# Decoder block on one Trainium2 core: q and k stored stacked and laid out by four DMAs a group, row maxima by way of DRAM, inverse of the softmax sums on ScalarE

## The chip, the cores and the metric

One core of a Trainium2 chip runs the whole program in one launch. The metric is the device time in microseconds (us); lower is better. Engines: PE is TensorE, ACT is ScalarE, DVE is VectorE, POOL is GpSimd, and SP is SyncE, which here only waits and issues DMAs.

## The reference, cut to what matters

```python
x = x + mixer(layernorm(x))                    # linear, conv, scan, gates; B=8, L=256, D=256
q = layernorm(x) @ WQ + bQ;  k = ctx @ WK + bK;  v = ctx @ WV + bV      # 16 heads of 16
scores = where(causal, einsum('bhqd,bhkd->bhqk', q, k) * SCALE, -inf)
x = x + (softmax(scores) @ v) @ WO + bO
x = x + top2_of_8_experts(layernorm(x))        # capacity 641 a expert, hidden 1024
```

The attention is exact in fp32 to a small tolerance. So q and k are held as two parts, high and low (`qkh`, `qkl`, type fp32r), and a product is high*high + high*low + low*high.

## The kernel before, in words

There are three stages: the mixer with the projections (`mixer_and_projections`), the attention with routing, and the experts (both in `attention_route_experts`). No scheduler works here: each engine has a queue written out by hand, and semaphores join them.

At the end of the mixer, q and k of each block of 512 tokens go to DRAM: `store` (L262) writes the high part to `qd[0]` or `kd[0]` and the low part to `qd[1]` or `kd[1]`, one DMA of 512 KB each. The stage ends when SP has seen all of them land (L309 to L312).

The attention works on 16 groups (GR). A group is one batch of 256 tokens and 8 of the 16 heads. For each group SP does two things:

- `lay(g)` (L1074) fills `q3` and `k3`. Per head they hold 48 rows: for q the parts high, high, low, for k high, low, high, so that one matmul of 48 rows gives the three products. Six 16-row pieces of q and six of k are loaded, each by a DMA of its own (L1082): 12 DMAs a group. `ITEMS` is 4 buffers, and `lay(g)` waits until group g-4 is used up (semaphore `st`).
- `maxima(g)` (L1085) waits for the row maxima in `mt` (semaphore `ml`) and writes them, again as high and low, into two extra rows of `q3`, one head a DMA (L1091): 16 DMAs of 1 KB a group. With -1 in the two extra rows of `k3` the next product has the maximum already subtracted.

The compute engines walk through steps t, three per group, 48 in all (NS). PE at step t does in this order: `turned_mask(t)` (L1375, waits for the exponential of t-1), `mask(u)` (L1350) and `scores(u)` (L1363) with u = t + LEAD and LEAD = 6, between these two `turned(t)` (L1389, keys by queries, 50 rows), and `weigh(t-1)` (L1411, probabilities times v and times ones). `turned(3g)` is the only one that waits for the maxima of group g. DVE reduces the scores of u to maxima (`maxima`, L1574). `turn_maxima(g)` on PE (L1424), `maxima_high` on ACT (L1248) and `maxima_low` on DVE (L1578) bring them into row form at step 3g-3. ACT computes the exponential (`exps`, L1243) of step t into one of three buffers `pr`. There is one PSUM buffer for the turned scores and one for the scores. After step 3g+2 of a group DVE divides (`divide`, L1583 and L1586): a reciprocal of the sums, then a product.

Every six steps a batch is projected (`project`, L1439); every twelve steps a block of four groups is normed (`normed`, L1253), turned (L1451), and gets logits (L1462), the choice of experts (`choose`), ranks (`ranks`, `place`) and its scatters to the experts' buffers in DRAM (`scatter` on POOL, L1173). The numbers NORM, TURN, LOGITS, RANKS, SEND in L998 are the steps at which this is due. The experts start when all scatters have landed.

## Time and profile before

| | |
|---|---|
| median of 3 runs | 905.03 us (902.49 to 905.58) |
| profiled execution, own time | 904.72 us |
| its span, first to last instruction | 903.0 us |
| mean granted PE clock | 0.858 |
| PE busy | 678.1 us (75%) |
| DVE busy | 508.2 us (56%) |
| ACT busy | 346.5 us (38%) |
| POOL busy | 325.3 us (36%) |
| DMA packets, bytes | 65987, 76.81 MB |

The page gives busy time by engine, the busy share in 40 slices, and the chain of work that ended last, followed back from the last instruction. SP has no row of busy time; what it does shows only in the chain and in the timeline, as "SPq" with a line number. Times in the timeline count from the first instruction. A clock of 1.00 is the upper level of PE (2.4 GHz), 0.50 the lower (1.2 GHz).

### The profile page before, as it was taken

What the parts mean: (1) busy time and instruction counts of PE and PEld (TensorE: products, weight loads), DVE (VectorE), ACT (ScalarE), POOL (GpSimd) and SP (SyncE); (2) the same over time, 40 slices, a digit from 0 to 9 for tenths busy, and PEclk for the clock granted to TensorE, in tenths of its full rate; (3) what the DMA queues carried; (4) which work ended last, traced back from release to release, by engine and by line L of the source; (5) the groups of instructions that cost most, each with busy time, mean ns of one, the idle gap of its engine ahead of it and who ended that gap; (6) DMA issues with size and microseconds to landing.
All of it is one profiled execution on the core that took longest, in us unless ns stands there. A gap on an engine that the chain in (4) does not pass through costs nothing.

```text
span 903.0 us, 13776 instructions
## 1 busy us (share of the span) xinstructions
PE 678.1 (75%) x4984; PEld 561.2 (62%) x4984; DVE 508.2 (56%) x985; ACT 346.5 (38%) x674; POOL 325.3 (36%) x307
## 2 busy tenths in 40 slices
PE   3869989798642357667667857733999999999992
PEld 2548877687431134344344535423999999999992
DVE  6686877869431224444544533422678777787741
ACT  4555647244310022223223213112556556565541
POOL 1326232423007000001113013052457776866855
PEclk9889999999875566879977878755999999999997
DMA  9002056211213632222323311115043454351213
GB/s 293 16 25 94 24 189 211 97 48 52 88 46 95 198 109 57 60 75 57 92 53 112 89 50 58 31 32 186 1 130 62 107 144 96 75 144 17 31 20 40
DMA packets 65987, 76.81 MB, mean 85 GB/s; under 512 B 17739, under 2 KB 52566, under 8 KB 65920
## 3 DMA queue, kind: packets, MB, share of 16 engines
q1 hardware_dynamic: 56704, 68.12, 23.8%
q0 software_dynamic: 9216, 7.81, 6.1%
q8 instruction: 40, 0.66, 0.3%
q14 instruction: 27, 0.22, 0.1%
HBM read 47.75 MB, written 29.64 MB: 86 GB/s over the span
## 4 chain that ended last, share of the span: by engine, by line
SPq 28%; PE 28%; issue 6%; POOL 4%; DMA 2%; DVE 1%; ACT 1%; POOLq 0%
SPq L1091 17%; PE w_bank L1516 13%; PE w_bank L101 11%; SPq L1082 10%; POOL out L1197 2%; PE w_bank L1485 1%; DMA a_q<-a_mt 1%; POOL a_k L1204 1%; POOL disp L1173 1%; POOL w_hl L1186 1%; DMA w_rows<-disp 1%; PE a_turned L1389 0%; DMA out<-w_y,w_to 0%; PE a_out L1411 0%; PE a_shared L1462 0%
## 5 line engine op out<-in xcount | busy, mean ns | idle before, releaser
L1574 DVE TENSOR_REDUCE a_nm<-a_scores 128x4 f32<-128x1024 f32 (+1 forms) x48 | 58.6, 1221 | 158.4 <-PE a_scores L1363 158.4
L1243 ACT ACTIVATE a_pr<-a_turned 128x1024 f32<-128x1024 f32 x48 | 49.2, 1025 | 197.5 <-PE a_turned L1389 197.5
L1516 PE MATMUL w_bank<-w_w2h,w_hh 128*108 128x256 f32 x384 | 108.6, 283 | 1.3 <-POOL w_hl L1186 1.3
L1516 PE MATMUL w_bank<-w_w2h,w_hl 128*108 128x256 f32 x384 | 107.8, 281 | 0.0
L1516 PE MATMUL w_bank<-w_w2l,w_hh 128*108 128x256 f32 x384 | 107.5, 280 | 0.0
L1677 DVE SCALAR_TENSOR_TENSOR w_v<-w_th,w_bank 128x324 f32<-128x324 f32 x128 | 62.8, 492 | 70.2 <-ACT w_th L1281 68.4
L1180 POOL TENSOR_TENSOR w_w1l<-w_s,w_w1h 128x256 fp32r<-128x256 f32 x64 | 56.7, 886 | 120.1 <-ACT w_w1h L1270 120.1
L1281 ACT ACTIVATE w_th<-w_bank 128x324 f32<-128x324 f32 x128 | 56.6, 443 | 99.8 <-PE w_bank L101 98.0
L1389 PE MATMUL a_turned<-a_q,a_k 50*128 50x256 f32 (+1 forms) x256 | 33.2, 364 | 81.9 <-DMA a_q<-a_mt 81.9
L1186 POOL TENSOR_TENSOR w_hl<-w_v,w_hh 128x324 fp32r<-128x324 f32 x64 | 56.5, 882 | 91.4 <-ACT w_hh L1287 91.4
L1389 PEld LDWEIGHTS a_turned<-a_q,a_k 50*128 50x128 f32 x256 | 22.3, 228 | 99.4 <-DMA a_q<-a_mt 90.2
L101 PE MATMUL w_bank<-w_xh,w_w1h 128*128 128x324 f32 x256 | 80.5, 315 | 1.1 <-ACT w_xh L1276 1.1
L101 PE MATMUL w_bank<-w_xh,w_w1l 128*128 128x324 f32 x256 | 80.1, 313 | 0.0
L1197 POOL DMA_INDIRECT out<-w_y,w_to x48 | 75.4, 1570 | 13.2 <-issue 9.9
L101 PE MATMUL w_bank<-w_xl,w_w1h 128*128 128x324 f32 x256 | 80.1, 313 | 0.0
L1653 DVE TENSOR_TENSOR w_w2l<-w_s,w_w2h 128x256 fp32r<-128x256 f32 x64 | 66.2, 1035 | 2.2
L1516 PEld LDWEIGHTS w_bank<-w_w2h,w_hh 128*108 128x108 f32 x384 | 65.8, 171 | 1.8 <-issue 1.8
L1516 PEld LDWEIGHTS w_bank<-w_w2l,w_hh 128*108 128x108 f32 x384 | 66.0, 172 | 0.0
L1516 PEld LDWEIGHTS w_bank<-w_w2h,w_hl 128*108 128x108 f32 x384 | 65.9, 172 | 0.0
L1287 ACT ACTIVATE w_hh<-w_v 128x324 fp32r<-128x324 f32 x128 | 60.3, 472 | 12.0 <-DVE w_v L1677 11.0
L101 PE MATMUL m_bank<-m_sh,m_wh 128*128 128x512 f32 x112 | 46.6, 416 | 10.3 <-ACT m_sh L422 6.9
L1173 POOL DMA_INDIRECT disp<-w_x,w_si x32 | 31.7, 990 | 58.8 <-DVE w_si L1646 46.3
(211 smaller groups left out, 1686.3 us busy)
## 6 DMA issues: line engine op xcount, KB each, us to landing
w_s<-in_L_ffn_w SPq DMA_DIRECT2D x16, 1024.0 KB, 5.0
a_q<-qd SPq DMA_DIRECT2D x96, 64.0 KB, 3.2
a_k<-kd SPq DMA_DIRECT2D x96, 64.0 KB, 2.3
disp<-c_blank SPq DMA_DIRECT2D x8, 658.1 KB
w_rows<-disp SPq DMA_DIRECT2D x8, 658.1 KB
vd<-m_vf SPq DMA_DIRECT2D x4, 1024.0 KB, 4.5
a_v<-vd SPq DMA_DIRECT2D x8, 512.0 KB, 4.2
a_q<-a_mt SPq DMA_DIRECT2D x256, 1.0 KB
```

Source lines behind the costliest of these rows:

```text
L101: mm = pe.matmul(out, a, b, start=first and n == 0, stop=last and n == 3 * len(parts) - 1)
L1082: sp.dma_start(m[at:at + HD, :, :].bitcast(F32), heads[e])\
L1091: sp.dma_start(q3[g % ITEMS][at:at + 1, p, :].bitcast(F32), mt[g % 2][h:h + 1, n, :].bitcast(F32))\
L1180: pool.tensor_tensor(w1_piece(w1l, f), w1_piece(s1[e % 2], f), w1_piece(w1h, f).bitcast(F32), ALU.subtract)\
L1186: pool.tensor_tensor(hl[:, g % 3, half(1)], v[:, n % 4, :], hh[:, g % 3, half(1)].bitcast(F32), ALU.subtract)\
L1197: pool.indirect_dma_start(out=out, out_offset=bass.IndirectOffsetOnAxis(ap=to[:, e % 3, t:t + 1], axis=0), in_=y[e % 2][:, t, :], in_offse ...
L1281: act.activation(th[:, n % 2, :], hb[n % 3][:, 0:HALF], ACT.Tanh, scale=0.5).then_inc(F["th"], 1)
L1287: act.activation(hh[:, g % 3, half(u)], v[:, n % 4, :], ACT.Copy).then_inc(F["hh"], 1)
L1516: mm = pe.matmul(eb[t // 2][0:SP_, (t % 2) * D:(t % 2 + 1) * D], a[:, g % 3, s], w2_piece(b, f), start=f == 0 and t % 2 == 0 and n == 0, s ...
L1574: dve.tensor_reduce(dst, src, AX.X, ALU.max).then_inc(A["nm"], 1)
L1653: dve.tensor_tensor(w2_piece(w2l, f), w2_piece(s2[e % 2], f), w2_piece(w2h, f).bitcast(F32), ALU.subtract)\
L1677: dve.scalar_tensor_tensor(v[:, n % 4, :], th[:, n % 2, :], 1.0, hb[n % 3][:, 0:HALF], ALU.add, ALU.mult).then_inc(F["v"], 1)
```

## The change

- In DRAM, q and k are now stacked as `lay` wants them: `qd` and `kd` have 3*D rows, and `store` writes high, high, low (q) or high, low, high (k), for two halves of 64 partitions: 6 DMAs of 256 KB in place of 2 of 512 KB, the high or the high and low part twice over. The weights' columns are reordered on the host (`by_pair`), so that the heads fall in the right place.
- `lay(g)` loads 48 rows at once: 4 DMAs of 192 KB in place of 12 of 64 KB.
- `maxima(g)` writes `mt` to a DRAM tensor `md` with one DMA, waits for it, and reads it back into the rows of `q3` with two DMAs of 2 rows: 3 in place of 16.
- LEAD is 7 in place of 6, and `turn_maxima`, `maxima_high` and `maxima_low` of group g come at step 3g-4 in place of 3g-3. LOGITS is 21 (was 20), RANKS 24 (23), SEND 25 (24).
- The inverse of the sums is made by ACT (`inverse`): a logarithm, then an exponential of minus that. DVE keeps the product.
- `values` and `store_base` are issued at other groups by SP.

```diff
@@ store
-                    for m, part in enumerate((qkh, qkl)):
-                        sp.dma_start(dst[m][:, i * BLK:(i + 1) * BLK].rearrange("(k p) t -> p k t", p=P),
-                                     part[:, :, :].bitcast(F32)).then_inc(S[sem], 16)
+                    for e in range(2):
+                        for n, part in enumerate((qkh, qkh, qkl) if dst is qd else (qkh, qkl, qkh)):
+                            sp.dma_start(dst.rearrange("(k e s q) n -> e s q k n", k=DC, e=2, s=3)[e, n][:, :, i * BLK:(i + 1) * BLK],
+                                         part[64 * e:64 * e + 64, :, :].bitcast(F32)).then_inc(S[sem], 16)
@@ lay and maxima, on SP
-                    for m, srcs in ((q3[g % ITEMS], (qd[0], qd[0], qd[1])), (k3[g % ITEMS], (kd[0], kd[1], kd[0]))):
-                        for n, src in enumerate(srcs):
-                            heads = src[k * P:(k + 1) * P, b * L:(b + 1) * L].rearrange("(p e r) t -> e r p t", p=4, e=2)
-                            for e in range(2):
-                                at = 64 * e + HD * n
-                                sp.dma_start(m[at:at + HD, :, :].bitcast(F32), heads[e])\
-                                    .then_inc(A[f"laid{g % ITEMS}"], 16)
+                    for m, src in ((q3[g % ITEMS], qd), (k3[g % ITEMS], kd)):
+                        rows = src.rearrange("(k e s r p) n -> k e (s r) p n", k=DC, e=2, s=3, r=HD)
+                        for e in range(2):
+                            sp.dma_start(m[64 * e:64 * e + 3 * HD, :, :].bitcast(F32), rows[k, e][:, :, b * L:(b + 1) * L])\
+                                .then_inc(A[f"laid{g % ITEMS}"], 16)
...
-                    for n in range(2):
-                        for e in range(2):
-                            for p in range(4):
-                                at, h = 64 * e + 3 * HD + n, 4 * e + p
-                                sp.dma_start(q3[g % ITEMS][at:at + 1, p, :].bitcast(F32), mt[g % 2][h:h + 1, n, :].bitcast(F32))\
-                                    .then_inc(A[f"m_in{g % 2}"], 16)
+                    sp.dma_start(md.rearrange("(g n h) t -> g h n t", n=2, h=8)[g], mt[g % 2][:, :, :].bitcast(F32)).then_inc(A["md"], 16)
+                    sp.wait_ge(A["md"], 16 * (g + 1))
+                    for e in range(2):
+                        at = 64 * e + 3 * HD
+                        sp.dma_start(q3[g % ITEMS][at:at + 2, :, :].bitcast(F32),
+                                     md.rearrange("(g n e p) t -> g e n p t", n=2, e=2, p=4)[g, e]).then_inc(A[f"m_in{g % 2}"], 16)
@@ ACT
+                def inverse(g):
+                    act.wait_ge(A["pv"], 3 * g + 3)
+                    ge(act, A["o"], g)
+                    act.activation(rc[:, :], obank[g % 2][:, L:2 * L], ACT.Ln).then_inc(A["ln"], 1)
+                    act.wait_ge(A["ln"], g + 1)
+                    act.activation(rc[:, :], rc[:, :], ACT.Exp, scale=-1.0).then_inc(A["rc"], 1)
...
+                act.preload_act_table_set("natural_log_exp_and_others")
                 maxima_high(0)
+                maxima_high(1)
                 for t in range(END):
+                    if t % 3 == 0 and 1 <= t // 3 <= GR:
+                        inverse(t // 3 - 1)
                     if t < NS:
                         exps(t)
-                    if t % 3 == 0 and t // 3 + 1 < GR:
-                        maxima_high(t // 3 + 1)
+                    if t % 3 == 2 and (t + 4) // 3 < GR:
+                        maxima_high((t + 4) // 3)
@@ DVE, divide
-                    dve.wait_ge(A["pv"], 3 * g + 3)
-                    step(dve.reciprocal(rc[:, :], obank[g % 2][:, L:2 * L]))
-                    settled()
+                    dve.wait_ge(A["rc"], g + 1)
```

The same shift from `t % 3 == 0` to `t % 3 == 2` stands for `turn_maxima` on PE and `maxima_low` on DVE. How the queues read now is shown at three places.

ACT, from the start of the attention into group 2: first before, then the change. `a_pr` is the exponential, `a_mt` the maxima, `a_rc` the inverse, `w_w1h` a piece of an expert's weight.

```order
L1248 ACTIVATE a_mt<-a_shared 8x256 [waits a_mT]
L1243 ACTIVATE a_pr<-a_turned 128x1024 [waits a_st]
L1248 ACTIVATE a_mt<-a_shared 8x256 [waits a_mT]
L1243 ACTIVATE a_pr<-a_turned 128x1024 [waits a_st] x2
L1270 ACTIVATE w_w1h<-w_s_0 128x2x128 [waits f_s1_0]
L1243 ACTIVATE a_pr<-a_turned 128x1024 [waits a_pv,a_st]
L1248 ACTIVATE a_mt<-a_shared 8x256 [waits a_m_in0,a_mT]
L1243 ACTIVATE a_pr<-a_turned 128x1024 [waits a_pv,a_st] x3
```

```order
L1306 ACT_TABLE_LOAD
L1248 ACTIVATE a_mt<-a_shared 8x256 [waits a_mT] x2
L1243 ACTIVATE a_pr<-a_turned 128x1024 [waits a_st] x3
L1248 ACTIVATE a_mt<-a_shared 8x256 [waits a_md,a_mT]
L1277 ACTIVATE w_w1h<-w_s_0 128x2x128 [waits f_s1_0]
L1253 ACTIVATE a_rc<-a_out 128x256 [waits a_pv]
L1255 ACTIVATE a_rc<-a_rc 128x256 [waits a_ln]
L1243 ACTIVATE a_pr<-a_turned 128x1024 [waits a_pv,a_st] x3
L1248 ACTIVATE a_mt<-a_shared 8x256 [waits a_md,a_mT]
```

The two instructions on `a_rc` stand ahead of the first exponential of the next group, and they wait for `a_pv`, the last products of the group before.

SP, one group in the steady part: first before, then the change.

```order
L1082 DMA a_q_1<-qd 16x4x256 [waits a_st]
L1082 DMA a_q_1<-qd 16x4x256 x5
L1082 DMA a_k_1<-kd 16x4x256 x6
L1091 DMA a_q_3<-a_mt 1x16x16 [waits a_ml]
L1091 DMA a_q_3<-a_mt 1x16x16 x15
```

```order
L1081 DMA a_q_1<-qd 48x4x256 [waits a_st]
L1081 DMA a_q_1<-qd 48x4x256
L1081 DMA a_k_1<-kd 48x4x256 x2
L1086 DMA md<-a_mt 8x2x256 [waits a_ml]
L1090 DMA a_q_3<-md 2x1024 [waits a_md]
L1090 DMA a_q_3<-md 2x1024
```

28 DMAs have become 7, and a wait on a DMA (`a_md`) stands inside.

PE in the change, the first step of a group: where `turned` waits for the maxima, and what stands between it and the next exponential.

```order
L1400 MATMUL a_turned<-a_q_1,a_k_1 128x256 [waits a_m_in1]
L1400 MATMUL a_turned<-a_q_1,a_k_1 128x256 x3
L1374 MATMUL a_scores<-a_k_3,a_q_3 128x256 x4
L1422 MATMUL a_out<-a_pr,a_v_0 32x128 [waits a_exp]
L1422 MATMUL a_out<-a_pr,a_v_0 32x128 x3
L1422 MATMUL a_out<-a_pr,a_ones 32x128 x4
L1422 MATMUL a_out<-a_pr,a_v_0 32x128 x4
L1422 MATMUL a_out<-a_pr,a_ones 32x128 x4
L1386 MATMUL a_turned<-c_identb,c_mask 128x2x128 [waits a_exp]
```

The transposes of the maxima (L1424 before) no longer stand in this step; they have moved to the step ahead of it, the third step of the group before.

## Rows read from the trace of the kernel before

**Rows 1.** The page, part 4: the chain that ended last, by line

```profile
SPq L1091 17%; PE w_bank L1516 13%; PE w_bank L101 11%; SPq L1082 10%; POOL out L1197 2%; PE w_bank L1485 1%; DMA a_q<-a_mt 1%; POOL a_k L1204 1%; POOL disp L1173 1%; POOL w_hl L1186 1%; DMA w_rows<-disp 1%; PE a_turned L1389 0%; DMA out<-w
```

**Rows 2.** Timeline of SP, one group: start, duration, queue, line, DMA, count

```profile
402.35 2.82 SPq L1082 DMA_DIRECT2D a_q<-qd  x6
...
408.84 9.99 SPq L1091 DMA_DIRECT2D a_q<-a_mt  x16
418.87 3.59 SPq L1082 DMA_DIRECT2D a_q<-qd  x6
```

**Rows 3.** Timeline of PE, one group without a wait for SP (idle time in brackets)

```profile
419.94 0.50 PE L1389 MATMUL a_turned<-a_q,a_k 50*128 50x256 f32 x4 [3.39 <-DMA a_q<-a_mt]
...
424.29 0.50 PE L1389 MATMUL a_turned<-a_q,a_k 50*128 50x256 f32 x4
...
426.08 1.99 PE L1439 MATMUL a_shared<-w_wo,a_ot 128*128 128x256 f32 x8
427.91 1.85 PE L1462 MATMUL a_shared<-w_rw,w_xt 128*128 128x8 f32 x16
429.62 0.59 PE L1375 MATMUL a_turned<-c_identb,c_mask 128*128 128x512 bf16 x2
...
430.36 0.66 PE L1389 MATMUL a_turned<-a_q,a_k 50*128 50x128 f32 x8
...
432.24 0.39 PE L1375 MATMUL a_turned<-c_identb,c_mask 128*128 128x256 bf16 x2
```

**Rows 4.** Stretches: busy (xcount) of PE, PEld, DVE, ACT, POOL; PE clock, DMA share, GB/s

```profile
409.00:412.00 3.00, 0.53 (x7) 0.33 (x4) 1.50 (x3) 1.50 (x4) 0.00 (x0) 1.00 0.15 44
421.00:423.00 2.00, 2.00 (x36) 1.67 (x35) 1.64 (x2) 1.46 (x4) 0.00 (x0) 0.50 0.39 110
280.00:300.00 20.00, 8.14 (x40) 4.26 (x40) 6.51 (x6) 0.37 (x1) 8.56 (x4) 0.50 0.47 144
320.00:572.00 252.00, 175.37 (x1768) 112.60 (x1768) 112.83 (x219) 63.69 (x89) 31.96 (x30) 0.79 0.27 73
```

**Rows 5.** Timeline of PE: the turn of a normed block

```profile
411.68 0.66 PE L1451 MATMUL a_shared<-c_ident,w_x 128*128 128x128 f32 x4 [2.47 <-ACT w_x L1253]
```

**Rows 6.** Groups of the page, ACT and DVE (busy us, mean ns | idle)

```profile
L1574 DVE TENSOR_REDUCE a_nm<-a_scores 128x4 f32<-128x1024 f32 (+1 forms) x48 | 58.6, 1221 | 158.4 <-PE a_scores L1363 158.4
L1243 ACT ACTIVATE a_pr<-a_turned 128x1024 f32<-128x1024 f32 x48 | 49.2, 1025 | 197.5 <-PE a_turned L1389 197.5
...
L1281 ACT ACTIVATE w_th<-w_bank 128x324 f32<-128x324 f32 x128 | 56.6, 443 | 99.8 <-PE w_bank L101 98.0
```

**Rows 7.** Timelines of SP and PE, end of the mixer and start of the attention

```profile
266.69 0.47 SPq L265 DMA_DIRECT2D qd<-m_qkl  x1
...
278.81 2.68 SPq L1082 DMA_DIRECT2D a_q<-qd  x6
...
286.25 1.12 PE L1363 MATMUL a_scores<-a_k,a_q 48*128 48x128 f32 x8 [14.35 <-DMA a_k<-kd]
...
300.62 0.79 PE L1363 MATMUL a_scores<-a_k,a_q 48*128 48x256 f32 x4
...
320.45 0.80 PE L1389 MATMUL a_turned<-a_q,a_k 50*128 50x256 f32 x4 [16.68 <-DMA a_q<-a_mt]
```

**Rows 8.** DMA landings: page part 6 (KB, us to landing), and one in the chain

```profile
a_q<-qd SPq DMA_DIRECT2D x96, 64.0 KB, 3.2
...
kd<-m_qkl SPq DMA_DIRECT2D x4, 512.0 KB, 3.9
...
434.73 1.64 DMA a_q<-a_mt
```

**Rows 9.** Timelines of PE and DVE, the last group; the chain at the first product

```profile
571.53 0.80 PE L1389 MATMUL a_turned<-a_q,a_k 50*128 50x256 f32 x4 [2.40 <-DMA a_q<-a_mt]
...
582.48 1.76 DVE L1583 RECIPROCAL a_rc<-a_out 128x256 f32<-128x256 f32 x1 [3.76 <-PE a_out L1411]
...
625.60 3.43 PE w_bank L101 x12
```

60 lines of the change are left out of this document (33 added, 27 removed).

## The prediction

> **What bounds the kernel now.** I read the chain that ended last first. SP's queue is the largest holder of the span: L1091 and L1082, the DMAs of the maxima and of q and k, hold 17% and 10% of it [rows 1], some 245 us. No other work of the attention is over 1%. The timeline of SP shows why: one group takes 6 issues for q in 2.82 us, as many for k up to 408.8, and 16 for the maxima in 9.99, with no idle time between, and the next group's first issue comes 16.5 us after this one's [rows 2]. So SP's own issuing is the bound: some 0.47 us an issue for a 64 KB piece, 0.62 us for a 1 KB row. The other engines wait: PE stands 3.39 us before the first product of a group until the maxima have landed [rows 3]. The attention proper, from the first `turned` at 320.45 [rows 7] to that of the last group at 571.53 [rows 9], is 251.1 us for 15 groups, 16.7 each. The mixer and the experts do not hang on this queue.
>
> The second thing to read is what a group costs once SP does not hold it. The timeline of PE has one that runs from its first product to the next group's masks with hardly a pause [rows 3].
>
> **What the change removes.** 28 issues a group become 7. The four large ones I take at 0.47 us; the issue time hardly follows the bytes, since the 512 KB store is issued in 0.47 too [rows 7]. The three for the maxima take 0.6 each. SP then needs 1.9 + 1.8 us and one landing between, 6 to 8 us a group [rows 8], and is no longer the bound. What is late next is PE.
>
> **Three steps of PE, at the upper clock.** Second step: from `turned` at 424.29 to the projection at 426.08, 1.79, plus the masks ahead of the next `turned`, 429.62 to 430.36, 0.74: 2.53. Third step: 430.36 to 432.24, 1.88, plus 0.74: 2.62. First step: 419.94 to 424.29, 4.35, but of this some 2.7 us ran at clock 0.50 [rows 4]; at 1.00 these are 1.35, so 3.0. Together 8.2 us [rows 3].
>
> **What the change adds on this path.** `inverse` stands on ACT ahead of `exps(3g+3)`, and it waits for the 32 small products of step 3g+2, the last thing PE does in that step. Before, that exponential ran beside those products. Now PE has nothing left: after the products come about 0.1 us to reach ACT, the logarithm, the exponential, the next exponential of 1024 columns at 1.02 [rows 6], and 0.15 back. No row shows a logarithm of 256 columns. Two rows of ACT give the slope: 443 ns for 324 columns and 1025 for 1024 [rows 6], 0.83 ns a column, so 0.39 for 256. Both ends: 0.3 and 0.45 each. I take 0.4 twice, and so 2.1 us of standing PE a group. On DVE 1.76 us of reciprocal [rows 9] go away, 16 times. That is 28 us of an engine with idle time, and I cost it at nothing: its reduces take 1.22 us each [rows 6], and what hides them is PE's work of a step.
>
> **The rest of the steps.** A projection is 1.83 us (426.08 to 427.91) and the logits 1.71 (to 429.62) [rows 3]. The turn of a normed block is twice 0.5 with a wait of 2.47 for ACT [rows 5] and some 0.4 for the second half: 3.9. Up to the last group these are 7 projections, 3 logits, 3 turns and 0.6 of ranks: 12.8 + 5.1 + 11.7 + 0.6 = 30.2, or 2.0 a group. So the **period is 8.2 + 2.1 + 2.0 = 12.3 us** in place of 16.7.
>
> **The maxima's way.** With LEAD 7 and `turn_maxima` at 3g-4, four steps lie between it and `turned(3g)`: the rest of one (1.0), a first step with its pause (5.1), a second and third (5.2) and masks (0.7), 12.0 us without projections. Needed are 1.9 for the copy and the subtraction (which stands behind a reduce), 0.6 to issue, a landing in DRAM, 1.2 for two issues, a landing in SBUF. Landings run from 1.64 (a 1 KB row) over 3.2 (64 KB of q) to 3.9 (512 KB written to DRAM) [rows 8]. That is 7.0 to 11.5; I take 8.5, hidden. The four loads of `lay` sit just ahead in the same queue, which argues for the upper half.
> The Trainium skill (page "DMA: Bandwidth & Descriptors", section on the anatomy of one DMA) speaks against the detour: a DMA has a fixed cost of about 2.0 us, most of it the receipt of the last write, worst where HBM is written; two trips would be 4.0 or more, which by its figure also leaves them hidden. No row here shows a small write to DRAM.
>
> **The start.** The last store of q is 6 issues in place of 2: four more at 0.47, +2 us before the mixer can end (at least 0.8, at most 4.5 if the bytes, 1.5 MB for 1, count in full). POOL's memsets follow as before, so `lay(0)` starts at 280.8. Four issues (1.9) and a landing near 3.2 give the first scores at 285.8, where they were at 286.25 [rows 7]. Steps run there at clock 0.50 [rows 4], and 5 of them took 14.37 us (286.25 to 300.62), 2.87 each. Seven are 20.1, so the first `turned` comes at 306.0 in place of 320.45. The other stores of the mixer double their high part behind some 2 us more of issue. The next writer of `qkh` asks for them more than 8 us later, so I cost them at nothing; without that cover it would be 2 us a block.
>
> **The end.** In the last group the inverse of group 14 stands ahead of an exponential, +2.1, and 0.8 us of ACT replace 1.76 on DVE, -0.9: +1.2. Ranks and scatters one step later fall into idle time of POOL.
> Two table loads are new on ACT. One falls under POOL's memsets. The other stands ahead of the experts' first tanh, while PE works on the first product for 3.43 us [rows 9], so nothing.
> By the Trainium skill ("ScalarE: Activation LUTs", what ACT_TABLE_LOAD costs) a switch is about 2.66 us, still under that; its price is on no row here.
>
> **The sum.** Last group's `turned` at 306.0 + 15 x 12.3 = 490.5, in place of 571.5: -81.0, and +1.2 at the end: -79.8. From the profiled execution's own 904.72 that gives **825 us**. The median of the three runs is 905.03, 0.3 above it, which I leave out.
>
> **The rivals.**
>
> *The low clock stays in the period* (20%). Today PE drops to 0.50 after its long pause in a group: idle before 419.94, it runs at 0.50 from 421 to 423, while the 2.47 us pause before 411.68 left it at 1.00 [rows 3 to 5]. The new pauses are 2.1 to 2.5, like the one that did no harm; that speaks against it. Several of them close together, with micro-pauses in the 50-row products, speak for it. If one low stretch of 2.7 us a group stays, it costs 1.35 or, with projections in it, up to 1.8: period 13.7 to 14.1, 846 to 852 us.
> The Trainium skill ("TensorE: Matmul & The Clock Gate", Part 1) says that the clock follows how busy PE has lately been, down to half when idle; by that rule denser work should end the drops and give the 825, and the pause of 2.47 us agrees with it.
>
> *The maxima are late after all* (8%). If both landings take 4.5 or more behind the loads, 12.7 to 16 are needed and the period grows by 1 to 2.5: 840 to 863 us. PE would again wait for the DMA at the first `turned` of a group.
>
> *More falls into the shadow* (5%). The 2.1 us pause also lets DVE, ACT and the norm's chain catch up, so that the 2.9 us waits of the turns and the masks' waits vanish, and some masks are already issued: period 11.2, 808 us.
>
> *The change does not relieve SP* (1%). If an issue were priced by its rows, 48 for 16, four would cost 1.41 each, 5.6 as today, and SP would need 5.6 + 1.8 + 3: 10.4, still under 12.3. Only with waits behind full queues on top does it bind, near 16: 880 to 903.
>
> *Slower: the pauses keep PE at the lower clock* (3%). In the first 20 us of the attention short bursts with pauses ran at 0.50 throughout [rows 4]. At 0.50 in every step, the 8.2 become 16.4 and the 1.1 of projections and logits in the 2.0 double: 21.6 a group, 15 x 9.3 = 140 more than the sum, 965 us. It needs a period of 17.6 to be slower than before, 5.3 over mine on 9.4 of PE's work, so the low level for over half of the time. Today, with longer pauses, the mean over the attention is 0.79 [rows 4], the low level for 42% of it.
>
> **The numbers.** The forecast has 63%, within 813 to 840: the period from 11.6 (some of the waits above shared) to 13.1, the start up to 3 us later. The range takes in the low clock: **812 to 857**. About 0.3%, 2.7 us, is what a measurement of this kernel can tell from no change. Faster 0.96, same 0.01, slower 0.03.
>
> **What would show it.** Right: SP's two lines have left the chain, and PE or ACT hold it between 306 and 490; the first product of a group follows the last by 12 to 13 us; ACT's logarithm waits for the small products, and PE's mask of the next step waits for the exponential, about 2 us, 16 times; `turned` has no wait for a DMA. Wrong: `turned` waits for the read of `md`, or the clock in the attention is under 0.8, or the period is over 14 or under 11.5; a first product far from 306 would show a fault in the start.

## The result and the profile after

| | before | after |
|---|---|---|
| median of 4 runs | 905.31 us (902.49 to 906.53) | 837.47 us (833.26 to 845.19) |
| the profiled execution, its span | 904.72 us, 903.0 | 833.26 us, 831.5 |
| mean granted clock of PE | 0.858 | 0.891 |
| first `turned` of the first and of the last group, us | 320.45, 571.53 | 312.55, 501.38 |
| period of a group (from first `turned` to the next group's, mean of 15) | 16.74 | 12.59 |
| from the last group's first `turned` to the end | 331.5 | 330.1 |

The ratio is 0.926, with a 95% interval of 0.918 to 0.935: 7.4% faster, or 67.8 us between the medians. Forecast were 825 (812 to 857). Of the 71.5 us between the two spans, 7.9 were won at the start, 62.3 in the period and 1.3 behind. The four runs of the change lie further apart (1.4%) than those of before (0.4%), and their mean clocks, 0.891 and 0.887 for the two at 833, 0.880 for 841.5 and 0.876 for 845.2, fall as the times rise.

The page of after, the chain by engine and by line, against [rows 1]:

```profile
PE 46%; issue 5%; POOL 4%; ACT 4%; DVE 3%; DMA 2%; SPq 2%; another core or an unknown queue 1%; POOLq 0%; ACTq 0%
PE w_bank L1527 14%; PE w_bank L101 12%; PE a_out L1422 5%; PE a_turned L1400 3%; PE a_turned L1386 2%; PE a_shared L1450 2%; POOL out L1197 2%; ACT a_pr L1243 2%; PE a_scores L1361 1%; PE a_scores L1374 1%; SPq L1081 1%; PE w_bank L1496 1%; PE a_shared L1473 1%; DVE a_nm L1585 1%; DMA md<-a_mt 1%
```

SP's two lines held 27% of the span; all of SP now holds 2%. In their place stand PE's own products of the attention (L1422, L1400, L1386).

Timeline of SP in after, one group and the next group's loads, against [rows 2]:

```profile
403.31 1.19 SPq L1081 DMA_DIRECT2D a_q<-qd  x2
404.54 1.25 SPq L1081 DMA_DIRECT2D a_k<-kd  x2
405.83 0.50 SPq L1086 DMA_DIRECT2D md<-a_mt  x1
409.37 0.54 SPq L1090 DMA_DIRECT2D a_q<-md  x2
416.94 1.19 SPq L1081 DMA_DIRECT2D a_q<-qd  x2
```

Four loads take 2.5 us (0.62 each, not 0.47), the maxima 0.50 and 0.54, and between write and reads lie 3.0 us of waiting for the landing. From 403.31 to 409.91 SP is at it, and then it stands idle for 7.0 us.

Timeline of PE in after over the same group, against [rows 3] (the first row, from the group before, is for comparison with that of 411.15):

```profile
399.49 0.64 PE L1422 MATMUL a_out<-a_pr,a_v 128*32 128x256 f32 x8
...
406.08 0.50 PE L1400 MATMUL a_turned<-a_q,a_k 50*128 50x256 f32 x4
...
409.69 0.39 PE L1386 MATMUL a_turned<-c_identb,c_mask 128*128 128x256 bf16 x2 [1.86 <-ACT a_pr L1243]
...
411.15 1.08 PE L1422 MATMUL a_out<-a_pr,a_v 128*32 128x256 f32 x8
```

The 3.39 us in front of a group's first product, for the maxima, are gone. In their place is a pause of 1.86 us behind the small products, and after it eight products take 1.08 us that take 0.64 at 399.49: PE has fallen to the lower clock (0.51 from 410.5 to 414.0). Not every such pause is followed by a fall: the row at 399.49 stands behind one of 1.86 us too, that of the group before, and there the clock stayed up. The timeline of ACT shows what fills it:

```profile
407.89 0.38 ACT L1253 ACTIVATE a_rc<-a_out 128x256 f32<-128x256 f32 x1 [3.24 <-PE a_out L1422]
408.31 0.42 ACT L1255 ACTIVATE a_rc<-a_rc 128x256 f32<-128x256 f32 x1
408.63 1.00 ACT L1243 ACTIVATE a_pr<-a_turned 128x1024 f32<-128x1024 f32 x1
```

Logarithm 0.38, exponential of 256 columns 0.42, then the exponential that PE waits for. The waits of the whole execution, of PE and of ACT (us in total, times, longest), say how often this is so:

```profile
PE a_turned L1386 <- ACT a_pr L1243: 31.1, 16, 4.3
...
ACT a_rc L1253 <- PE a_out L1422: 48.1, 15, 4.9
```

Fifteen of PE's 16 waits are the inverse's: 14 of 1.86 to 1.91 us, and one of 4.30 ahead of 491.68, where ACT's logarithm began 2.5 us after the last product, held by something that the trace calls only "remote". The sixteenth, 0.69, is in the first group, where no inverse stands ahead yet.

Stretches of after, against [rows 4] (busy of PE, PEld, DVE, ACT, POOL, then PE's clock, DMA share, GB/s):

```profile
290.00:300.00 10.00, 5.71 (x30) 3.25 (x30) 3.67 (x3) 0.00 (x0) 3.83 (x2) 0.50 1.01 232
300.00:312.00 12.00, 7.78 (x36) 3.32 (x34) 5.72 (x6) 0.74 (x2) 0.00 (x0) 0.50 0.86 269
320.00:470.00 150.00, 122.61 (x1448) 79.09 (x1446) 71.33 (x157) 58.00 (x94) 21.65 (x21) 0.92 0.37 100
```

In the attention the clock rose to 0.92, so PE is at 0.50 for some 16% of the time in place of 42%; the low stretches have not gone. The start ran as low as before.

The start, in the timelines of SP and PE of after, against [rows 7]:

```profile
266.57 1.23 SPq L266 DMA_DIRECT2D qd<-m_qkh  x2
...
268.58 2.54 SPq L266 DMA_DIRECT2D qd<-m_qkh  x2
271.17 1.18 SPq L266 DMA_DIRECT2D qd<-m_qkl  x1
284.07 1.26 SPq L1081 DMA_DIRECT2D a_q<-qd  x2
...
290.31 1.11 PE L1374 MATMUL a_scores<-a_k,a_q 48*128 48x128 f32 x8 [13.14 <-DMA a_k<-kd]
...
303.05 0.50 SPq L1086 DMA_DIRECT2D md<-a_mt  x1
310.71 0.56 SPq L1090 DMA_DIRECT2D a_q<-md  x2
...
312.55 0.80 PE L1400 MATMUL a_turned<-a_q,a_k 50*128 50x256 f32 x4 [1.74 <-DMA a_q<-md]
```

Three things are seen. The six issues of q's last store take 5.8 us, 1.0 each. The first scores come 6.2 us after the first load is issued, in place of 7.4. And the first write of maxima, 16 KB issued at 303.05, lets its reads go only at 310.71: it lies behind 2 MB of the first expert's weights, while the DMA engines are busy for 0.86 to 1.01 of the time.

### The profile page after: what moved, and what is told of

It reads as the page before. It is cut to its first block, busy times and chain, and to the rows that moved or that the text cites. A ratio compares the mean times of both kernels' runs of the same rounds, so it can differ in the third digit from the quotient of the medians.

```text
span 831.5 us, 13504 instructions
## 1 busy us (share of the span) xinstructions
PE 658.1 (79%) x4984; PEld 547.4 (66%) x4984; DVE 478.9 (58%) x969; ACT 359.5 (43%) x708; POOL 325.2 (39%) x307
## 4 chain that ended last, share of the span: by engine, by line
PE 46%; issue 5%; POOL 4%; ACT 4%; DVE 3%; DMA 2%; SPq 2%; another core or an unknown queue 1%; POOLq 0%; ACTq 0%
PE w_bank L1527 14%; PE w_bank L101 12%; PE a_out L1422 5%; PE a_turned L1400 3%; PE a_turned L1386 2%; PE a_shared L1450 2%; POOL out L1197 2%; ACT a_pr L1243 2%; PE a_scores L1361 1%; PE a_scores L1374 1%; SPq L1081 1%; PE w_bank L1496 1%; PE a_shared L1473 1%; DVE a_nm L1585 1%; DMA md<-a_mt 1%
## 5 line engine op out<-in xcount | busy, mean ns | idle before, releaser
L1197 POOL DMA_INDIRECT out<-w_y,w_to x48 | 75.3, 1570 | 13.1 <-issue 9.9
L101 PEld LDWEIGHTS w_bank<-w_xh,w_w1h 128*128 128x128 f32 x256 | 48.6, 190 | 1.4 <-ACT w_xh L1283 1.4
L101 PEld LDWEIGHTS w_bank<-w_xl,w_w1h 128*128 128x128 f32 x256 | 48.8, 190 | 0.0
```

The costliest lines, as they stand in the source:

```text
L101: mm = pe.matmul(out, a, b, start=first and n == 0, stop=last and n == 3 * len(parts) - 1)
L1197: pool.indirect_dma_start(out=out, out_offset=bass.IndirectOffsetOnAxis(ap=to[:, e % 3, t:t + 1], axis=0), in_=y[e % 2][:, t, :], in_offse ...
```

## The experiments

Ten kernels besides the two, and the changed one again, in three sessions. Each session also timed the kernel before, at 901.4, 904.5 and 901.9 us; where kernels of different sessions are compared, it is by their ratio to that. The last session ran the changed kernel again; the mean of its two ratios, 0.926 and 0.921, is 0.924, and a thousandth is 0.9 us.

| kernel | us | ratio to before (95%) | first `turned` | period | clock 320 to 470 us |
|---|---|---|---|---|---|
| before | 905.3 | 1 | 320.5 | 16.74 | 0.79 |
| change | 837.5 | 0.926 (0.918 to 0.935) | 312.6 | 12.59 | 0.92 |
| change again | 831.3 | 0.921 (0.918 to 0.924) | 311.6 | 13.07 | 0.88 |
| inverse behind | 800.8 | 0.888 (0.887 to 0.890) | 311.5 | 10.60 | 0.99 |
| reciprocal on DVE | 822.6 | 0.913 (0.911 to 0.915) | 310.7 | 11.70 | 0.94 |
| pause filled | 816.4 | 0.906 (0.903 to 0.908) | 312.1 | 11.63 | 1.00 |
| 16 DMAs for maxima | 850.9 | 0.943 (0.938 to 0.949) | 317.0 | 13.73 | 0.83 |
| 12 DMAs for q and k | 850.0 | 0.940 (0.935 to 0.945) | 327.6 | 13.11 | 0.80 |
| steps alone | 899.9 | 0.995 (0.993 to 0.997) | 319.8 | 16.47 | 0.80 |
| steps of before | 829.8 | 0.917 (0.912 to 0.922) | 314.0 | 12.72 | 0.88 |
| third trip | 843.2 | 0.930 (0.926 to 0.934) | 312.8 | 13.35 | 0.84 |
| start | 796.1 | 0.881 (0.878 to 0.884) | 303.8 | 10.83 | 0.93 |
| start and weights | 799.9 | 0.885 (0.883 to 0.887) | 303.7 | 11.07 | 0.97 |

First `turned` and period (from there to that of the last group, by 15) are read from the timeline of PE of one execution each, as is the clock; behind the last group's first product all of them need 327 to 333 us. The mixer does not end at the same time in every execution either: SP's first issue of q's last store lies between 263.9 and 268.5 us in kernels whose mixer is the same (266.57 in the change, 263.89 in its second execution). So small differences in the first `turned` say little, and below it is counted from that issue or from the first load where it matters. The times of the kernel with the steps of before lie from 822.5 to 835.3, and its profile is of the longest.

### The two halves of the change

**The maxima by 16 DMAs again.**

```diff
-                    sp.dma_start(md.rearrange(...)[g], mt[g % 2][:, :, :].bitcast(F32)).then_inc(A["md"], 16)
-                    sp.wait_ge(A["md"], 16 * (g + 1))
-                    for e in range(2):
-                        at = 64 * e + 3 * HD
-                        sp.dma_start(q3[g % ITEMS][at:at + 2, :, :].bitcast(F32), md.rearrange(...)[g, e]) ...
+                    for n in range(2):
+                        for e in range(2):
+                            for p in range(4):
+                                at, h = 64 * e + 3 * HD + n, 4 * e + p
+                                sp.dma_start(q3[g % ITEMS][at:at + 1, p, :].bitcast(F32), mt[g % 2][h:h + 1, n, :].bitcast(F32)) ...
```

> The changed kernel with the maxima of a group carried by the 16 small DMAs from SBUF to SBUF again, and q and k still by 4. Theory (an issue on SP costs about 0.6 us whatever it carries, and what counts is SP's sum against PE's period of 12.6): 16 x 0.62 + 4 x 0.62 = 12.4 us a group, at the bound; 0 to 15 us slower than the change, 837 to 853, with SP idle for less than 1 us a group. So nearly the whole gain is had without the detour. Rival (the detour itself is the gain: small writes into SBUF rows are slow to land, or block the queue): the time goes back up by 40 or more, to 877 or over.

Measured: 0.943, some 17 us over the change by the ratios, a little over the 15 that I had given as the most. The timeline of SP in this kernel:

```profile
384.32 10.80 SPq L1090 DMA_DIRECT2D a_q<-a_mt  x16
395.17 0.58 SPq L1095 DMA_DIRECT2D a_v<-vd  x1
395.79 1.21 SPq L1081 DMA_DIRECT2D a_q<-qd  x2
397.05 1.25 SPq L1081 DMA_DIRECT2D a_k<-kd  x2
398.34 10.76 SPq L1090 DMA_DIRECT2D a_q<-a_mt  x16
```

SP has no idle time: 13.4 us from the first load to the next group's without a load of v, 14.0 with one (every second group), and the period is 13.73. The mechanism holds: SP is the bound again, and PE waits for the maxima in five groups between 320 and 460 us, 7.5 us in all. The period is 0.7 to 1.1 us over the change's, which is 10 to 17 us. The first `turned` is 4.5 us later too, but 2.0 of that is the mixer, which ended later in this execution (its issue is at 268.52, for 266.57).

**q and k by 12 DMAs again.**

```diff
-    LAID = 16 * 4
+    LAID = 16 * 12
...
-                        for e in range(2):
-                            sp.dma_start(m[64 * e:64 * e + 3 * HD, :, :].bitcast(F32), rows[k, e][:, :, b * L:(b + 1) * L]) ...
+                        for n in range(3):
+                            for e in range(2):
+                                at = 64 * e + HD * n
+                                sp.dma_start(m[at:at + HD, :, :].bitcast(F32), rows[k, e][HD * n:HD * (n + 1), :, b * L:(b + 1) * L]) ...
```

> The changed kernel with q and k of a group laid by 12 DMAs of 16 partitions again (from the stacked tensors), and the maxima still through DRAM by 3. Theory: SP issues 12 x 0.47 to 0.62 + 1.8 = 7.5 to 9.2 us a group and waits for one landing of 3 us: 10.5 to 12.2, just under the period of 12.6; 0 to +8 us against the change, 837 to 846. Rival (the pieces themselves are faster as 64 partitions, by their landing or by the load on the DMA engines): 20 or more slower. With the run of 16 small maxima it divides the gain: if each half alone has nearly the whole gain, it was SP's sum that had to fall under PE's period, and neither half matters by itself.

Measured: 0.940, 15 us over the change, where I had expected 8 at most. The period is 13.11, that of the change in its second execution (13.07). The place is the start, where the first write of maxima goes out at 322.63 and not at 303.05. Timelines of SP and PE of this kernel:

```profile
318.80 3.78 SPq L1083 DMA_DIRECT2D a_k<-kd  x6
322.63 0.50 SPq L1089 DMA_DIRECT2D md<-a_mt  x1
...
327.62 0.80 PE L1403 MATMUL a_turned<-a_q,a_k 50*128 50x256 f32 x4 [10.64 <-DMA a_q<-md]
```

Four groups are laid before that write, with 8 issues more each, some 20 us. PE waits 10.6 us for it once. In the middle SP has room (3.0 us of idle time up to 397.50, 4.5 up to 412.84). The write of the maxima lets its reads go after 2.0 us there (379.35 to 381.39), where the change needs 3.5 (405.83 to 409.37; 3.1 to 4.2 in most other groups). It stands behind the same bytes, but those were issued over 8.7 us here and over 2.5 there. That this is the reason is argued, not shown.

So each half alone, with the rest of the change in place, wins 51 to 54 us, both 69: the gain belongs to neither. What had to happen was that SP's sum fell under PE's period, and either half does nearly that. The rival of an issue priced by its rows is out: in these two kernels an issue takes 0.63 us with 16 partitions (3.78 by 6), 0.62 with 48 (1.25 by 2), and 0.67 with one row of 1 KB (10.80 by 16).

**The order of the steps, alone and undone.** The first is the kernel before with the lead of seven, the earlier turn of the maxima and the later logits and ranks; the second the change with those of before. The core of both:

```diff
-    LEAD = 6
-    PROJECT, BOTH, NORM, TURN, LOGITS, RANKS, SEND = 8, 14, 16, 17, 20, 23, 24
+    LEAD = 7
+    PROJECT, BOTH, NORM, TURN, LOGITS, RANKS, SEND = 8, 14, 16, 17, 21, 24, 25
...
-                    if t % 3 == 0 and 0 <= t // 3 + 1 < GR:
-                        turn_maxima(t // 3 + 1)
+                    if t % 3 == 2 and 0 <= (t + 4) // 3 < GR:
+                        turn_maxima((t + 4) // 3)
```

> The kernel before with only the order of the steps taken from the change: the scores seven steps ahead in place of six, the turn of the maxima and its copies one step earlier, logits, ranks and scatters one step later, loads of v and stores of x placed accordingly. All DMAs and the reciprocal as before. Theory: SP's issues (28 a group, 16.7 us) bound it as before, and an earlier order of PE's work gives nothing: within 3 us of the kernel before. Rival (part of the gain is the longer lead, which hides the way of the maxima): 10 or more us faster than the kernel before.

> The changed kernel with the order of the steps from before: scores six steps ahead, the turn of the maxima only three steps before the first product that needs them, logits, ranks and scatters one step earlier. The DMAs and the inverse as in the change. By the prediction's sum the way of the maxima needs 8.5 us and would have 12.0 - 3.3 = 8.7 left. Theory: PE now waits for the read of md in some groups, 0 to 1.5 us each: 0 to 20 slower than the change, less some 3 us at the start, where one step less is run ahead. Rival (the detour has so much room that the order does not matter): within 3 us of the change.

Measured: alone 4 to 5 us of gain (0.995, with 0.993 to 0.997), a little more than I gave it and far from the rival's ten. Undone, 0.917 against 0.921 for the change on the same chip, with overlapping intervals: nothing. No product of that kernel waits for a DMA between 320 and 460 us. By my sum the way of 8.5 us fitted into the 8.7 that were left by 0.2, and I gave the misses that such a margin makes up to 20 us; there are none. The rival was right: with the detour the order of the steps is worth nothing that shows.

**A third trip for the maxima.**

```diff
                     sp.wait_ge(A["md"], 16 * (g + 1))
+                    sp.dma_start(md2[16 * g:16 * (g + 1), :], md[16 * g:16 * (g + 1), :]).then_inc(A["md2"], 16)
+                    sp.wait_ge(A["md2"], 16 * (g + 1))
```

> The changed kernel with a third trip for the maxima: after the write to DRAM they are copied to a second place in DRAM, and only then read into the rows of q. It adds one issue and one landing of some 3 us to every group's way, and leaves everything else. Theory (the way was forecast with 3.5 us to spare, and the trace of the change shows some 7 us between the landing and the first product that needs it): in the middle of the attention nothing is lost, only the first groups, where the small transfers stand behind the 2 MB of weights, start 3 to 8 us later. 3 to 10 us slower than the change. Rival (the way is as long as the period allows): 3 us more a group, 35 to 50 slower.

Measured: 0.930, 6 us over the mean of the change's two ratios; its interval (0.926 to 0.934) lies inside that of the change's first measurement and above that of the second. The number fits; the place I had named hardly does. The third trip takes only the 2.1 us from 308.76 to 310.81:

```profile
308.76 0.52 SPq L1088 DMA_DIRECT2D md<-md  x1
310.81 0.56 SPq L1092 DMA_DIRECT2D a_q<-md  x2
```

The first `turned` comes at 312.80. From the first load, at 281.96, that is 30.8 us, where the change has 28.5 in its first execution and 30.2 in its second: 0.6 to 2.4 us, not 3 to 8. Between 320 and 460 us no product waits for a DMA here either. What differs from the first profile of the change is the clock, 0.84 against 0.92 and 0.88, and that varies in the change itself. So the rival (35 to 50 us) is out, and whether the trip costs anything stays open.

### The inverse and its pause

**Inverse behind the exponential.**

```diff
                 for t in range(END):
-                    if t % 3 == 0 and 1 <= t // 3 <= GR:
-                        inverse(t // 3 - 1)
                     if t < NS:
                         exps(t)
+                    if t % 3 == 0 and 1 <= t // 3 <= GR:
+                        inverse(t // 3 - 1)
```

> The changed kernel with one edit: on ACT the logarithm and the exponential of the inverse stand behind the first exponential of the next group, not ahead of it. Theory (PE's own chain is the bound now, and the inverse's wait for the 32 small products puts a pause of 1.86 us into it once a group): the pause goes, the period between first products of groups falls from 12.6 to between 10.7 and 11.3, and the time falls by 15 x 1.3 to 1.9 = 20 to 28 us, to 809 to 818. Rival A (the pause is shadow time in which DVE and the norm's chain catch up, so that its removal only moves the wait to the masks or to the turns of normed blocks): 0 to -8 us. Rival B (SP's round trip of the maxima through DRAM is next in line): first products of a group wait for a DMA, -5 to -15 us.

Measured: 800.8 us, 0.888, about 32 us under the change, more than the 28 that the pause could hold. The period is 10.60, 2.0 to 2.5 less than the change's, for a pause of 1.86. The timelines of PE and ACT in this kernel show the inverse beside PE's work:

```profile
397.36 0.39 PE L1386 MATMUL a_turned<-c_identb,c_mask 128*128 128x256 bf16 x2
```

```profile
397.50 0.38 ACT L1253 ACTIVATE a_rc<-a_out 128x256 f32<-128x256 f32 x1 [0.24 <-PE a_out L1422]
```

PE's mask at 397.36 has no bracket, and the logarithm waits 0.24 us and not 3 to 5. Behind the first group's no first product waits for a DMA, so rival B is out. Where did the rest of the gain come from? The next run was made for that.

**The pause filled, its length left.**

```diff
+                def fill(g):
+                    ge(pe, A["o"], g)
+                    for _ in range(5):
+                        pe.matmul(obank[(g + 1) % 2][:, :].rearrange("p (n k) -> p n k", n=4), c["mask"][:, :],
+                                  c["identb"][:, :].unsqueeze(1).to_broadcast([P, 4, P]), start=True, stop=True, ...)
...
                     if 1 <= t <= NS:
                         weigh(t - 1)
+                    if t % 3 == 0 and 0 < t < NS:
+                        fill(t // 3 - 1)
```

> The changed kernel with PE kept busy in the pause of 1.86 us: after the last small products of a group it does five products of 512 columns in bf16 whose result nobody reads (they go to the bank of the next group's sums, before that group starts), some 1.35 us at the upper clock; the inverse stays ahead of the exponential. The waits stay as long as they are. Theory (besides its own 1.86 us the pause also brings the low clock back, which is why taking it away gave 33 to 37 us and not 28): the clock between 320 and 470 us rises from 0.92 toward 0.98, and the time falls by 4 to 10 us. Rival A (the low stretches come from projections and the norm's turns): clock and time as in the change, within 3 us. Rival B (the filling is not hidden): up to 10 us slower.

Measured: 816.4 us against 831.3 for the change on the same chip, 15 us faster with five useless products more a group. Timeline of PE:

```profile
393.55 1.25 PE L1430 MATMUL a_out<-c_identb,c_mask 128*128 128x512 bf16 x5
395.48 0.39 PE L1386 MATMUL a_turned<-c_identb,c_mask 128*128 128x256 bf16 x2 [0.68 <-ACT a_pr L1243]
```

1.25 us of filling and 0.68 of waiting: the mask comes as late as in the change. But the stretch from 320 to 470 us is at the upper clock throughout. The same stretch of this kernel and, in a second fence, of the one with the inverse behind (the change's stands above, 0.92). As there, the clock is the number ahead of the last two:

```profile
320.00:470.00 150.00, 134.69 (x1625) 84.70 (x1625) 77.67 (x173) 62.25 (x101) 25.22 (x25) 1.00 0.37 105
```

```profile
320.00:470.00 150.00, 134.76 (x1704) 87.39 (x1702) 80.23 (x178) 71.11 (x113) 32.00 (x30) 0.99 0.42 113
```

The change and the filled kernel can also be laid side by side group by group, from first product to first product. Two groups of the change, then the same two of the filled kernel:

```profile
419.23:435.19 15.96, 13.36 (x123) 8.04 (x122) 6.88 (x18) 6.68 (x11) 8.09 (x7) 0.68 0.57 148
435.19:448.94 13.75, 11.55 (x138) 8.32 (x137) 5.77 (x8) 4.92 (x8) 3.66 (x4) 1.00 0.34 92
```

```profile
414.89:427.43 12.54, 10.17 (x127) 6.37 (x126) 6.79 (x18) 6.64 (x11) 8.11 (x7) 1.00 0.50 144
427.43:441.18 13.75, 12.74 (x142) 8.73 (x142) 5.77 (x8) 4.92 (x8) 3.66 (x4) 1.00 0.40 124
```

Seven of the change's 15 groups ran at 1.00 throughout, and they are as long as the filled ones to 0.02 us. Seven others had a mean clock of 0.68 to 0.89 and are 1.0 to 4.3 us longer, together 15.1, of which 2.4 is the one long wait of the inverse. The first group ran low in both. In the change's second execution 13 of the 15 are longer, by 0.6 to 3.1 us. So what the filling took away is, but for that one wait, the low stretches.

So the 32 us of the inverse are two things of about the same size. **The clock**: 15 us, which PE lost in low stretches behind the pause. **The pause itself**: from filled to behind, 0.906 to 0.888, 16 us, or 1.0 us a group of period (11.63 to 10.60), and not 1.86. The rest of it was shadow, my rival A in half. Eight groups are 1.76 to 1.80 us shorter than the filled ones, nearly the whole pause. Four win 0.65 to 1.31, three of them with a new wait of 1.11 for DVE's reduce, and one wins nothing. The first group loses 0.3, and one other loses 1.7, with a mean clock of 0.87 and these two waits of PE:

```profile
387.94 0.61 PE L1386 MATMUL a_turned<-c_identb,c_mask 128*128 128x512 bf16 x2 [1.24 <-ACT a_pr L1243]
390.46 0.60 PE L1361 MATMUL a_scores<-c_mask,c_identb 128*128 128x512 bf16 x2 [1.91 <-DVE a_nm L1585]
```

That the gain came near 15 x 1.86 was chance. Without the filled run I would have read it as the pause alone.

**Reciprocal on DVE again.** The diff is that of `divide` undone: `dve.reciprocal` behind the wait for `pv`, no `inverse` on ACT.

> The changed kernel with the inverse as a reciprocal of 256 columns on DVE again, no logarithm or exponential on ACT for it; the DMAs stay as in the change. Theory: ACT's pause of 1.86 us a group goes as in the run with the inverse behind, but DVE gets 1.76 us of reciprocal back, which stands ahead of the reduce of the next scores and of the copies; PE then waits at the masks for up to 0.6 us a group. 10 to 26 us faster than the change: 812 to 828. If it is as fast as the run with the inverse behind (within 3 us), DVE's reciprocal was free all along, as I had costed it. Rival: DVE with its reduces at 1.22 us is so close behind PE that the reciprocal costs its whole length: 0 to 5 us gained.

Measured: 822.6, 0.913: 9 us faster than the change, 22 slower than the inverse behind on ACT. A reciprocal takes 1.75 us. The chain by line:

```profile
PE w_bank L1525 15%; PE w_bank L101 13%; DVE a_nm L1583 3%; DVE a_rc L1592 3%; PE a_out L1420 2%; PE a_turned L1398 2%; POOL out L1197 2%; PE a_shared L1448 2%; SPq L1081 1%; PE a_turned L1384 1%; PE a_scores L1359 1%; PE w_bank L1494 1%; PE a_scores L1372 1%; PE a_shared L1471 1%; DMA md<-a_mt 1%
```

The reciprocal is 3% of the chain, 25 us; in before no such line stood there [rows 1]. The loss is not the same in every group. Between 340 and 476 us, set against the inverse behind, the six groups in which DVE has 2.7 to 4.1 us of work besides the attention's own are 0.9 to 3.4 us longer, the five with 1.4 to 2.3 us of it only 0.1 to 0.5. So moving it off DVE is worth 22 us, if ACT does it behind the exponential, and it cost 9 us where the change put it.

### The changed kernel again

> The changed kernel itself, unchanged, as the measure for the two runs beside it on the same chip. Its four times so far lie between 833.3 and 845.2 with mean clocks of 0.891 down to 0.876, the longer the lower. Theory (part of the low clock stayed in the attention and comes or goes from run to run): again a spread of over 1%, with time and clock in step, between 830 and 848. Rival (the spread was that one session's): all within 0.3% of one value.

Measured: 831.3 us (828.7 to 837.0), a spread of 1.0%, and again the longest of the four has the lowest clock (0.883), the shortest the highest (0.891); the two between them, 0.884 at 830.4 and 0.889 at 832.3, are not in that order. The kernels that keep the clock up do not scatter like this: 800.0 to 801.5 for the inverse behind, 815.3 to 817.7 for the filled pause. The kernel of the next part, whose clock was at 0.93, scatters by 0.8% (793.6 to 799.6). So the spread goes with the low stretches.

### The start

**Store shared, memsets awaited one by one.** With the inverse behind:

```diff
-                    for e in range(2):
+                    for e in range(1 if dst is qd and i == NBLK - 1 else 2):
...
+                act.wait_ge(S["ql"], DC * NBLK)
+                for n, part in enumerate((qkh, qkh, qkl)):
+                    act.dma_start(...[1, n][:, :, (NBLK - 1) * BLK:], part[64:128, :, :].bitcast(F32)).then_inc(S["q_st"], 16)
...
                 def lay(g):
+                    if g < ITEMS:
+                        sp.wait_ge(A["minus"], 2 * (g + 1))
...
-                sp.wait_ge(A["minus"], 2 * ITEMS)
                 lay(0)
```

> The changed kernel with the inverse behind the exponential, and two edits at the start of the attention: the last store of q is issued half by SP and half by ACT, three DMAs each, and SP waits for the two memsets of the buffer that it loads, not for all eight. Theory (six issues at about 1 us each hold up the end of the mixer by 2.5 to 3 us, and SP stands 6 us longer than it must behind POOL's memsets): first scores 8 to 9 us earlier than in the run with the inverse behind alone, time 790 to 794 where that had 800.8. Rival (the start is held by the landing of the small transfers behind the 2 MB of weights, whose place in the queue does not change): the first product that needs maxima moves less, by 3 to 5 us, 796 to 798.

Measured: 796.1 us, 0.881, the fastest of all. In us that is 2 over the forecast of 790 to 794 and inside the rival's range; but the kernel before, timed beside it, was 3.1 us slower than beside the inverse behind, and by the ratios it lies 7 us under the inverse behind, at 794. The place decides against the rival, which had the first product move by 3 to 5 us. The timelines of SP, ACT, POOL and PE:

```profile
264.40 1.22 SPq L266 DMA_DIRECT2D qd<-m_qkh  x2
264.41 1.90 ACTq L579 DMA_DIRECT2D qd<-m_qkh  x2
...
266.34 2.22 ACTq L579 DMA_DIRECT2D qd<-m_qkl  x1
...
272.88 7.93 POOL L1209 MEMSET a_k<- 32x1024 f32 x8 [18.82 <-POOLq L241]
...
274.85 1.25 SPq L1087 DMA_DIRECT2D a_q<-qd  x2
...
303.83 0.80 PE L1405 MATMUL a_turned<-a_q,a_k 50*128 50x256 f32 x4 [2.20 <-DMA a_q<-md]
```

The issues are over after 4.2 us and not 5.8, and the memsets start 8.5 us after the first issue, not 9.5: the split saved 1 us and not 2.5 to 3. The first load goes out 2 us after the memsets begin and not 8: the 6 us are there. The first `turned` comes at 303.83, 7.7 us earlier than with the inverse behind alone, whose last store began at the same time (264.49). It still waits 2.20 us for the maxima. Some 3 us are given back in the period (10.83 for 10.60), with the clock at 0.93 for 0.99.

**And the weights later.** In addition `weights(0)` goes behind the first group's maxima and `weights(1)` behind the second's, and the conversions of the first expert start four steps later on ACT, DVE and POOL.

```diff
                 values(1)
-                weights(0)
                 lay(3)
...
-                    if g == 0:
-                        weights(1)
+                    if g in (0, 1):
+                        weights(g)
```

> The run before this one, and in addition the first expert's 2 MB of weights are issued after the first group's maxima (the second's after the second group's), with their conversions on ACT, DVE and POOL four steps later. Theory (the write and the reads of the first maxima took about 7 and 2 us behind those 2 MB, PE stood 2.6 us for them): the first product that needs maxima comes when PE has done its seven steps ahead, 3 to 6 us earlier than without, so 785 to 790. Rival (the later conversions collide with the work of the steps, or the weights come late for them): no gain, or a few us lost.

Measured: 799.9 us, 0.885, 3.8 us slower than the run before it on the same chip, with intervals that just overlap, where 6 to 11 us less were expected. The wait for the DMA is gone: the write of the maxima went out at 294.95 and the reads at 298.63, 3.7 us later and not 8. From the first load at 276.86 to the first `turned` at 303.71 it is 26.9 us, where it was 29.0. That is 2 us and not 3 to 6, because the seven steps ahead, at 0.50, take until then by themselves: the first `turned` has no wait. It comes no earlier on the clock of the trace only because the mixer ended 2.5 us later in this execution (the issue at 266.94, for 264.40). The gain is lost in the period, 11.07 for 10.83, 3.6 us in all; the last four groups take 13.0, 10.0, 11.2 and 14.1 for 11.5, 9.8, 13.8 and 9.9. Whether that is the later conversions or the clock no run shows, and between 320 and 470 us the clock was the higher one here (0.97 for 0.93). So the rival was nearer, and whether the edit costs anything is open.

## Why the prediction was right, and where it was not

825 was forecast, 837.5 and 831.3 were measured, inside the range, and the main reason held: with SP's sum under PE's period, the period fell from 16.7 to PE's own chain. The two halves, each alone, show it. Step by step:

- **What bounded the kernel**: right. SP's lines left the chain.
- **28 issues become 7, and SP is no longer the bound**: right in kind, too cheap in its terms. A load of 48 partitions takes 0.62, not 0.47; the four 2.5, not 1.9. I had read the cheaper of two rows: the other six loads of q, at 418.87, took 3.59, or 0.60 each [rows 2]. With a sum of 6.6 under 12.6 it cost nothing here. It would where the margin is thin: the run of 16 small ones is over the bound by just such tenths.
- **The inverse's pause**: the mechanism, its place and its length are right, 1.86 for 2.1, 0.38 and 0.42 for 0.4 twice, 15 times, not the 16 that I wrote: the last group's inverse has no exponential behind it. Its worth is not what its length says: 1.0 in the period, and as much again by the clock.
- **"Three steps of PE, at the upper clock", 8.2, and "the rest of the steps", 2.0**: this is the step that failed in size, in two directions that cancel. With the pause there and the clock at 1.00 throughout, the filled run has a period of 11.63, not 12.3: my sum of waits and pieces is 0.7 too long. The change itself runs at 0.92 or 0.88 and needs 12.6 or 13.1, 1.0 to 1.4 more: the low stretches, but for 0.2 in the first that is the one long wait. That is the 1.35 of the rival that I gave 20%. The forecast and this rival were both half right, and the first came out near only since the sum under it was too long.
- **"The new pauses are 2.1 to 2.5, like the one that did no harm"**: wrong. I argued from one pause of 2.47 us that left the clock up. The run with the pause filled shows that pauses of 1.86 once a group bring low stretches with them, as after 409.69 above, though not in every group. The Trainium skill ("TensorE: Matmul & The Clock Gate", Part 1) says that the clock follows how busy PE has lately been; by that rule filling a pause can pay although nothing comes earlier by it, and the filled run agrees.
- **The maxima's way, 7.0 to 11.5, taken as 8.5, hidden**: right, it is hidden. Neither three steps in place of four nor a third trip makes a product wait. The rival of late maxima (8%) is out. The Trainium skill's fixed cost of about 2 us a DMA ("DMA: Bandwidth & Descriptors", the anatomy of one DMA), which that section gives for DMAs issued by GpSimd, while these are SP's, would make the write 2.0 and more. From its issue to the reads' it was 3.5, and 2.0 in the kernel with 12 loads; the trip from DRAM to DRAM took 2.1. The 3.5 lies in the upper half of the landings that I allowed for (1.64 to 3.9).
- **The start, 306.0**: wrong by 6.5 us, the largest error. Two terms: the mixer's end came 5.3 us later, not 2, since the six issues cost 1.0 each and not 0.47 (my bound of 4.5 for the bytes counted in full was nearer). And the first scores were 4.5 late for it and for the 6.2 us that the first load needed where I had 5.1; then the seven steps were ready at 310.8, and the maxima's landing took the 1.7 us left. The store's part is firm: from its first issue to POOL's memsets it is 9.5 us in both executions of the change, 4.6 before. In the second execution the mixer was done 2.7 us earlier, but the landing cost 3.0, and the first `turned` came at 311.62. I had costed the way in the steady state only, where the weights do not stand ahead.
- **The end, +1.2**: the spans show -1.3, and those of the ten other kernels behind their last group scatter from 327 to 333. The term is smaller than what can be seen.
- **"Two table loads are new on ACT", nothing**: right. The timeline of ACT in after has both, one at 276.11 under POOL's memsets, and one from 553.74 to 555.02, ahead of a tanh that waits longer for PE:

```profile
556.35 0.44 ACT L1288 ACTIVATE w_th<-w_bank 128x324 f32<-128x324 f32 x1 [1.33 <-PE w_bank L101]
```

  I wrote that no row has a price; the mixer's loads in the trace of before had it, 1283 ns each. One stands there with no idle time on either side:

```profile
100.40 0.63 ACT L416 ACTIVATE m_th<-m_cv 128x512 f32<-128x512 f32 x1 [1.20 <-DVE m_cv L791]
101.05 1.28 ACT L557 ACT_TABLE_LOAD   x1
102.34 1.15 ACT L470 ACTIVATE m_zh<-m_z 128x512 fp32r<-128x512 f32 x2
```

  From the end of the instruction ahead, at 101.03, to the start of the next, at 102.34, it is 1.31 us. The Trainium skill ("ScalarE: Activation LUTs", what ACT_TABLE_LOAD costs) gives about 2.66 us for a whole switch; these rows show half of it.
- **"On DVE 1.76 us of reciprocal go away, and I cost it at nothing"**: right for the sum, since I compared with a period that had the inverse on ACT; wrong as a statement on DVE. With SP out of the way, the reciprocal on DVE is worth 22 us, 1.1 a group and some 5 behind the last group's first product, against an inverse that nobody waits for. The cover that I named, PE's work of a step, is thin in the groups where DVE has more to do.
- **Rivals**: more in shadow (5%) at 808 did not come, though half the pause was shadow. SP not relieved (1%) and the low clock throughout (3%) are out, the latter for all but the start, where PE stays at 0.50 until the first `turned`.

In sum: the period was 0.3 to 0.8 a group longer than forecast (4 to 12 us), the start 6.5 later, the end 2.5 earlier, together 8.3 in the profiled execution (4.3 + 6.5 - 2.5). Two slips in the sums change nothing: 285.8 + 20.1 is 305.9, and projections and logits are 1.2 a group, not 1.1, in the rival of the low clock throughout. That the forecast came within 1.5% owes something to luck, since PE's work was put 0.7 us a group too long, where the low clock added 0.8 to 1.4.

## What to carry to other kernels

When a queue is the bound, compare its sum with the period of the engine behind it: the gain ends where the two meet, whichever part of the queue is cut, and the last tenths of an issue count only near that point. When work is moved from one engine to another, look at what stands behind it there: the same two operations are worth 32 us by standing behind the exponential and not ahead of it. And where a pause on TensorE is removed, its length says little about its worth: part of it is shadow, and part of the gain is the clock; a run that fills the pause with useless products tells the two apart.

## What the runs showed of the hardware that I had not expected

- Useless work made the kernel faster: 75 more products of 512 columns (five behind each of 15 groups, 1.25 us each time) and 15 us less, by keeping the granted clock at 1.00 where it had been at 0.88 to 0.92. Pauses of 1.86 us, once in 12 us or so, had been enough to lose it in 7 of 15 groups in one execution.
- A 16 KB write behind 2 MB of loads let its reads go 7.7 us after its issue, with the DMA engines busy 0.86 to 1.01 of the time; 3.7 with these loads moved behind it; 3.1 to 4.2 in most groups in the middle of the attention, and 2.0 in the kernel with 12 loads.
- A switch of ACT's table, with ACT busy on both sides of it, took 1.31 us.
- The issue of a store from 64 partitions to DRAM took 0.6 us alone and 1.2 with others ahead of it, 5.8 for six; half of them on a second queue shortened it only to 4.2.
- A DMA of 16 KB from DRAM to DRAM, and the wait for it, took 2.1 us.
